# FP4 quantiser of a block kernel: one threshold sum carries the sign sums, half and scale folded together

## The reference, cut to what matters

```python
xn = layernorm(x)                                  # 1024 features
s  = attn_ref(xn, ...)                             # linear attention, projection, MLP 1024 -> 2048 -> 1024
g  = silu(ffn_ref(xn, w_gate, w_up, w_down))       # every operand of the three products is quantised
out = x + s * g

_GRID = [0.0, 0.5, 1.0, 1.5, 2.0, 3.0, 4.0, 6.0]
_MID  = [0.25, 0.75, 1.25, 1.75, 2.5, 3.5, 5.0]
def fp4_quant_dequant(x):                          # blocks of 16 along the last dimension
    scale = max(max|xb| / 6, 1e-12)
    xn = xb / scale
    return _GRID[searchsorted(_MID, |xn|)] * sign(xn) * scale

def ffn_ref(x, w_gate, w_up, w_down):              # 1024 -> 2816 -> 1024
    h = silu(fp4_linear(x, w_gate)) * fp4_linear(x, w_up)
    return fp4_linear(h, w_down)
```

## Time and profile before

| | us |
|---|---|
| median of 2 runs | 6698.14 (6688.92 to 6707.36) |
| profiled execution | 6623.11 |
| its span, slowest core (3) | 6621.5 |
| spans of the other cores | 6599.9 to 6619.9 |
| mean granted TensorE clock, all cores | 0.696 to 0.698 |

### The profile page before, as it was taken

How to read it: one execution, slowest core, us unless ns; L and a number is a source line. 1 busy time by engine, 2 the same in 40 slices (tenths; PEclk the granted TensorE clock), 3 DMA queues, 4 the chain that set the end, 5 groups by cost and what they waited for, 6 DMA issues and landing times.

```text
span 6621.5 us, 58555 instructions; the slowest of 8 cores (6599.9 to 6621.5 us)
## 1 busy us (share of the span) xinstructions
PE 2592.5 (39%) x11098; PEld 1110.6 (17%) x11098; DVE 3878.3 (59%) x8760; ACT 2051.6 (31%) x4067; POOL 3.2 (0%) x13
## 2 busy tenths in 40 slices
PE   0167447642313133374004555522232322223298
PEld 0023113211101011132001222211111111111143
DVE  0500330133787777524987777758888888888522
ACT  0244224321322322222323334323333333333211
POOL 0000000000000000000000000000000000000000
PEclk9999678866656566687556767665666555665599
DMA  9420110014111111001112222230111110111255
GB/s 108 121 61 23 34 50 29 18 46 81 40 42 39 40 35 39 29 24 45 45 54 92 85 92 89 84 89 34 41 44 45 44 44 30 44 45 44 70 194 179
DMA packets 227699, 396.08 MB, mean 60 GB/s; under 512 B 147861, under 2 KB 147989, under 8 KB 217626
## 3 DMA queue, kind: packets, MB, share of 16 engines
q1 hardware_dynamic: 226778, 375.57, 17.6%
q0 software_dynamic: 576, 16.78, 2.3%
HBM read 246.44 MB, written 145.33 MB: 59 GB/s over the span
## 4 chain that ended last, share of the span: by engine, by line
PE 33%; issue 26%; DVE 20%; ACT 11%; SPq 5%; DMA 4%; DVEq 1%; ACTq 0%
PE gps L1093 6%; PE ups L1147 5%; PE kvg_ps L402 4%; PE d_ps L1249 4%; PE c1ps L937 3%; SPq L195 2%; PE c2ps L965 2%; PE q_ps L453 2%; PE prA L601 2%; DVE gld L1159 1%; PE xp4t L1179 1%; DMA xa<-x 1%; PE prB L601 1%; ACT qb_s L709 1%; ACT qb_u L712 1%
## 5 line engine op out<-in xcount | busy, mean ns | idle before, releaser
L1179 PE MATMUL xp4t<-ident_b,hq 128*128 128x128 bf16 x704 | 178.9, 261 | 1306.0 <-ACT hqf L1185 1256.2
L1147 PE MATMUL ups<-wquT,xqu 128*128 128x512 bf16 (+1 forms) x1536 | 364.2, 404 | 71.9 <-DMA xqu<-xqT_h 38.9
L917 PE MATMUL xp2t<-ident_b,xn 128*128 128x128 bf16 x256 | 65.0, 265 | 831.5 <-DVE xn L905 432.1
L1093 PE MATMUL gps<-wqgT,xqf 128*128 128x512 bf16 (+1 forms) x1536 | 377.0, 414 | 19.6 <-ACT xqf L1082 19.6
L1075 PE MATMUL xp3t<-ident_b,xq 128*128 128x128 bf16 x256 | 67.8, 265 | 765.2 <-DVE xq L742 736.1
L703 ACT ACTIVATE qb_sgn<-qb_u 128x704 f32<-128x704 f32 x128 | 101.0, 790 | 839.2 <-DVE qb_u L696 838.2
L362 DVE SCALAR_TENSOR_TENSOR xn<-xn,rstd_all,rep_s 128x1024 bf16<-128x1024 f32 x32 | 41.1, 1284 | 542.7 <-ACT xn L351 481.7
L1249 PE MATMUL d_ps<-wqdT,hln 128*128 128x512 bf16 x1408 | 313.6, 384 | 71.6 <-DMA hln<-hqT_h 54.2
L1159 DVE TENSOR_TENSOR gld<-gld,up 128x2816 f32<-128x2816 f32 x32 | 99.0, 3092 | 372.6 <-ACT up L1156 372.6
L1179 PEld LDWEIGHTS xp4t<-ident_b,hq 128*128 128x128 bf16 x704 | 73.8, 105 | 1409.1 <-issue 1408.3
L402 PE MATMUL kvg_ps<-qkvT,fmsup 128*128 128x512 bf16 x1024 | 275.9, 437 | 23.0 <-ACT fmsup L384 23.0
(11 more groups left out here) (243 smaller groups left out, 6709.8 us busy)
## 6 DMA issues: line engine op xcount, KB each, us to landing
xa<-x SPq DMA_DIRECT2D x160, 512.0 KB, 3.7
gate_h<-gate SPq DMA_DIRECT2D x32, 1408.0 KB, 5.6
gld<-gate_h SPq DMA_DIRECT2D x32, 1408.0 KB, 6.7
hqT_h<-hqf SPq DMA_DIRECT2D x32, 704.0 KB, 3.7
hln<-hqT_h SPq DMA_DIRECT2D x32, 704.0 KB, 5.5
out<-otl SPq DMA_DIRECT2D x32, 512.0 KB, 3.0
winw<-L_ffn_w_gate SPq DMA_DIRECT2D x22, 512.0 KB, 3.4
winw<-L_ffn_w_up SPq DMA_DIRECT2D x22, 512.0 KB, 3.4
```

The lines of the kernel that those rows point to most:

```text
L1093: S.add("pe", lambda pe, b=b, ic=ic, cgo=cgo, cgw=cgw, cgi=cgi: pe.matmul(g_ps[cgi % 4][:, 0:cgw], xqf[b][:, P * ic:P * (ic + 1)], wqgT[:, ...
L1147: S.add("pe", lambda pe, b=b, ic=ic, cgo=cgo, cgw=cgw, cgi=cgi: pe.matmul(u_ps[cgi % 4][:, 0:cgw], xqu[b][:, P * ic:P * (ic + 1)], wquT[:, ...
L1179: S.add("pe", lambda pe, b=b, ic=ic: pe.transpose(xp4_ps[ic % 2], hq[b][:, P * ic:P * (ic + 1)], ident_b[:]), waits=tw, inc="PE", ev="a2_t ...
```

## The change

Inside `quant_gen` only. The two sign instructions on VectorE (`sadd`, `smul`) move ahead of the four threshold counts. `smul` now forms s5+s6+2*s7. The first count, a `tensor_scalar`, becomes a `scalar_tensor_tensor` that adds this sum. The instruction that joined the counts with the sum (`tA3`) is gone. The factor one half goes into the product of sign and scale, which becomes a `scalar_tensor_tensor`, and the last instruction adds 4 instead of 2. Per unit VectorE has 8 instructions behind `u2` instead of 9, and a weight chunk has 30 steps instead of 31. Nothing changes on ScalarE, TensorE or in the DMAs.

```diff
@@ -712,8 +712,14 @@
             S.add("sc", lambda sc: sc.activation(s7, u2, AF.Sign, bias=thrB[:, 2:3]),
                   waits=[e("sgn")], inc="SC", ev=e("s7"))
             yield
-            S.add("v", lambda v: v.tensor_scalar(tA, u2, 0.0625, None, op.is_gt),
-                  waits=[e("u2")], inc="V", ev=e("tA1"))
+            S.add("v", lambda v: v.tensor_tensor(s5, s5, s6, op.add),
+                  waits=[e("s5"), e("s6")], inc="V", ev=e("sadd"))
+            yield
+            S.add("v", lambda v: v.scalar_tensor_tensor(s6, s7, 2.0, s5, op.mult, op.add),
+                  waits=[e("s7"), e("sadd")], inc="V", ev=e("smul"))
+            yield
+            S.add("v", lambda v: v.scalar_tensor_tensor(tA, u2, 0.0625, s6, op.is_gt, op.add),
+                  waits=[e("u2"), e("smul")], inc="V", ev=e("tA1"))
             yield
             S.add("v", lambda v: v.scalar_tensor_tensor(tB, u2, 0.5625, tA, op.is_gt, op.add),
                   waits=[e("tA1")], inc="V", ev=e("tB1"))
@@ -724,22 +730,13 @@
             S.add("v", lambda v: v.scalar_tensor_tensor(tB, u2, 3.0625, tA, op.is_gt, op.add),
                   waits=[e("tA2")], inc="V", ev=e("tB2"))
             yield
-            S.add("v", lambda v: v.tensor_tensor(s5, s5, s6, op.add),
-                  waits=[e("s5"), e("s6")], inc="V", ev=e("sadd"))
-            yield
-            S.add("v", lambda v: v.scalar_tensor_tensor(s6, s5, 0.5, s7, op.mult, op.add),
-                  waits=[e("s7"), e("sadd")], inc="V", ev=e("smul"))
-            yield
-            S.add("v", lambda v: v.scalar_tensor_tensor(tA, tB, 0.5, s6, op.mult, op.add),
-                  waits=[e("smul")], inc="V", ev=e("tA3"))
-            yield
             sb_ = sca.rearrange("p nb -> p nb ()").broadcast_to([P, nb, 16])
-            S.add("v", lambda v: v.tensor_tensor(
-                tB.rearrange("p (nb b) -> p nb b", b=16),
-                sgn.rearrange("p (nb b) -> p nb b", b=16), sb_, op.mult),
-                waits=[e("sgn"), e("tA3")], inc="V", ev=e("tBs"))
-            yield
-            S.add("v", lambda v: v.scalar_tensor_tensor(dst_ap, tA, 2.0, tB, op.add, op.mult),
+            S.add("v", lambda v: v.scalar_tensor_tensor(
+                tA.rearrange("p (nb b) -> p nb b", b=16),
+                sgn.rearrange("p (nb b) -> p nb b", b=16), 0.5, sb_, op.mult, op.mult),
+                waits=[e("sgn"), e("tB2")], inc="V", ev=e("tBs"))
+            yield
+            S.add("v", lambda v: v.scalar_tensor_tensor(dst_ap, tB, 4.0, tA, op.add, op.mult),
                   waits=[e("tBs")], inc="V", ev=done_ev)
 
         def run_gens(gens):
```

More of the change, by code:

```diff
@@ L726, in quant_gen @@
             yield
-            S.add("v", lambda v: v.tensor_tensor(s5, s5, s6, op.add),
-                  waits=[e("s5"), e("s6")], inc="V", ev=e("sadd"))
-            yield
-            S.add("v", lambda v: v.scalar_tensor_tensor(s6, s5, 0.5, s7, op.mult, op.add),
-                  waits=[e("s7"), e("sadd")], inc="V", ev=e("smul"))
-            yield
-            S.add("v", lambda v: v.scalar_tensor_tensor(tA, tB, 0.5, s6, op.mult, op.add),
-                  waits=[e("smul")], inc="V", ev=e("tA3"))
-            yield
-            sb_ = sca.rearrange("p nb -> p nb ()").broadcast_to([P, nb, 16])
-            S.add("v", lambda v: v.tensor_tensor(
-                tB.rearrange("p (nb b) -> p nb b", b=16),
-                sgn.rearrange("p (nb b) -> p nb b", b=16), sb_, op.mult),
-                waits=[e("sgn"), e("tA3")], inc="V", ev=e("tBs"))
-            yield
-            S.add("v", lambda v: v.scalar_tensor_tensor(dst_ap, tA, 2.0, tB, op.add, op.mult),
+            sb_ = sca.rearrange("p nb -> p nb ()").broadcast_to([P, nb, 16])
+            S.add("v", lambda v: v.scalar_tensor_tensor(
+                tA.rearrange("p (nb b) -> p nb b", b=16),
+                sgn.rearrange("p (nb b) -> p nb b", b=16), 0.5, sb_, op.mult, op.mult),
+                waits=[e("sgn"), e("tB2")], inc="V", ev=e("tBs"))
+            yield
+            S.add("v", lambda v: v.scalar_tensor_tensor(dst_ap, tB, 4.0, tA, op.add, op.mult),
                   waits=[e("tBs")], inc="V", ev=done_ev)
```

## The result

The changed kernel takes 6971.99 us in the median (6880.50 to 7012.17, 11 runs), the kernel before, run beside it, 6698.14 (10 runs, 6622.97 to 6779.58). The ratio is 1.0412, 95% interval 1.0324 to 1.0501. In some executions of either kernel the cores of one die or of both run at a lower granted clock and take longer, and the ratios leave the clearly longer ones out while the medians hold them all. Two more sets of runs of the same pair gave 1.0372 (1.0313 to 1.0431) and 1.0311 (1.0240 to 1.0382); the mean of the three, weighted by their intervals, is 1.036, some 240 us. The forecast was 224 us, a ratio of 1.033, 6922 us, with 6870 to 6968 as its range. Direction and mechanism were right, and so was the size of what the quantiser's stages lose; the two medians of this set are 274 us apart, and the changed kernel's lies 4 us above the range.

A forecast was written before the change was run, and what follows sets the result against it. No engine bounds the whole; loops of waits between engines set the gate and up stages, VectorE the weight and MLP stages. 18 + 36 + 113 + 57 = +224 us on 6698 gives 6922 us, range 6870 to 6968.

The forecast's parts named there:

- The gate stage: Gate stage: six more instructions of 0.604 us behind the sign sum's wait, 3.62 us a tile, +113 us in all.
- the bare stall: Quantiser pairs: VectorE waits at the sign sum for ScalarE's Signs, 1.99 us per 704 pair, 1.68 per 512 pair.
- the ring: Gate stage loop: sign sums and following VectorE work, transposes, matmuls, Silus, Signs; the early counts sat free in VectorE's wait.
- The up stage: Up stage: the first pair of 32 tiles pays 1.12 us net each, +36 us.
- the cover of the second pair: Up stage: the second pair's 1.12 us hides in 9.63 us of idle time; uncovered it would add another 36.
- rival 3: TensorE's clock: longer pauses slow all gate matmuls, +26 us, as much again in the up stage; 6974 us, chance 6%.
- The weight stage: Weight stage: all 16 pairs lie on the path and pay 1.12 us net each, +18 us.
- The MLP stage: MLP stage with chunks: 44 pairs at 1.1 us, +49, plus shifted portion ends; together +57 us.
- 15 counted places: MLP stage: 30-step chunks shift where portions end; terms +20, +8, -12, -3 and -6 us.
- Rival 1: Quantiser: Signs are ready in time, so the shorter VectorE program wins 72 us; 6626 us, chance 3%.
- Rival 2: Gate stage: the loop has slack, so the six extra instructions cost nothing, 112 us drop out; 6810 us, chance 5%.
- the last one: Whole kernel: adds 224 us to the runs' median 6698, 76 us above the profiled span of 6621.5, giving 6922.

The follow-up runs named there:

- gate_stage_only: Against the kernel before: the changed order in the gate stage's quantiser alone, the old one elsewhere; gate stage 910.7 us (+113.7).
- product_first: Against the changed kernel: same eight instructions, product of sign and scale put ahead of the sign sums; ratio to the kernel before 1.0042.
- arrival_order: Against the kernel before: counts stay ahead, then the product of sign and scale, then s5, s6, s7 added one by one as they arrive; ratio 0.9938.
- load_ahead_new: both_rings_open_new plus x of tile t+2 loaded ahead of tile t's stores in the gate stage; 6359.04 us, kernel before 6737.22.
- both_rings_open_new: Changed kernel with gate Signs ahead of the previous tile's Silus and up-stage transposes and copies ahead of the next tile's product and quantiser; ratio 0.9852.
- whole_again: The changed kernel run once more, unaltered, for a second profile and ratio against the kernel before; 6915.09 us, ratio 1.0372.
- moved_only: Against the kernel before: only the two sign instructions moved ahead of the counts, all nine instructions and the old arithmetic kept; ratio 1.0492.
- load_ahead_old: both_rings_open_old plus x of tile t+2 loaded ahead of tile t's stores in the gate stage; 6116.55 us, kernel before 6737.22.
- both_rings_open_old: Kernel before with gate Signs ahead of the previous tile's Silus and up-stage transposes and copies ahead of the next tile's product and quantiser; ratio 0.9536.
- all_but_gate: Against the kernel before: the changed order everywhere except in the gate stage's quantiser; ratio 1.0164.
- signs_before_silu_old: Kernel before with the gate stage's quantiser of tile t+1 put ahead of tile t's matmuls and Silus; ratio 1.0001, gate stage 789.1 us.

## Why the prediction was right, and where it was not

**The gate stage** (+113 computed, +113.4 to +113.8 measured) held in each step: the sum waits for ScalarE in 32 of 32 tiles, 331 us against "some 320", tiles 29.0 us apart as written, and the sum's start still set by the Signs. `gate_stage_only` shows the term by itself, `product_first` and `arrival_order` that it goes by the instructions behind the wait, `load_ahead_new` that it falls to the bare stall when the ring is opened.

**The up stage** (+36 computed, +45 measured). The stall (1.91 us, computed 1.99) and its net price (1.18 for 1.12 a tile) were right, and so was the cover of the second pair, shown by `both_rings_open_new`. The under-sized part lies ahead of the product: from the first `ups` matmul to the product a tile takes 12.10 us in place of 11.84, 8 us over the stage. The rows of the `ups` matmuls have 364.2 us busy, 404 ns each, before and 373.3, 411 ns, in the first profile after: TensorE's matmuls themselves. This is rival 3 with a small price: I had ruled that the mix of clock levels would stay, and in the gate stage it did (a burst of 48 is 11.78 us in the mean in both kernels). In the up stage it did not: over the 32 bursts of core 3 the granted clock was 0.84 in the mean before, 0.83 in `whole_again` and 0.79 in `moved_only`, and the bursts took 11.38, 11.59 and 12.13 us.

**The weight stage** (+18 computed, +19.4): 30.5 us of waits in 16 pairs, "16 x 2.0 = 32" was expected.

**The MLP stage** (+57 computed, +50.2 measured) was a sum of 44 plain stalls (49) and of 15 counted places where a portion ends (8 net; the terms as written add up to 56, not 57). The total is inside the 40 to 80 that I had set as its test, but no run took one counted place by itself. The plain stalls alone would give 49. `moved_only`, whose chunks keep their 31 steps, grew by 80.8 here; less the 44 removed L715 (44 x 0.68 = 30) that is 51, what the changed kernel grew by. This speaks for places that came to nothing in the sum; whether my count is right in its parts is open.

**The rivals.** Rival 1 (the shorter program wins) needed the `s6` ready within 0.87 us and found it 1.9 late; it becomes true in the up and weight stages of `product_first`, where other work stands in front of the wait. The Trainium skill (Perfetto Trace Analysis, "Identifying the Most-Contended Engine") tells to optimise the engine of highest occupancy first. Here that engine had 104 us less to do and the kernel took some 240 us longer; `load_ahead_old`, with VectorE's work as before (3870 us busy), took 513 us less than the 4910 between attention and down by having waits taken away. Rival 2 fell with the gate stage.

**VectorE's busy time** fell by 104 us, not 134. I had scaled up the busy times of L715's rows, 0.95 and 0.75 us a pair, but each pair overlaps the start of the next one: by their steps in the timeline (0.87 and 0.68 us a pair, which the path's sums used) it is 80 x 0.87 + 76 x 0.68 = 121. The last 17 us are not accounted for.

**The step that failed is the last one**: "The median of the runs is 76 us above that span; I add the same 224 to it", and with it the upper end of the range, 6968, which holds 26 us for the clock and 20 for the MLP count and nothing for the spread of the runs (the lower end has 9). The 224 held, and the base happened to hold: the kernel before, run beside the changed one, has the very median of 6698.14 that the sum started from. What did not hold is that the changed kernel's median would lie the same 76 us above the span that the sum gives: in this set it lies 127 us above the computed 6845, though the profiled spans of `whole_again` (6818.5 to 6863.8 on its cores) are where the sum puts them. That the base was right was luck: the two runs I had, 6688.92 and 6707.36, are among those ten and happen to be the middle two, and they lay close together by chance. In five sets of runs the median of the kernel before was 6653.57, 6669.51, 6698.14, 6730.79 and 6737.22, and its single executions went from 6617 to 6799, and the changed kernel's medians were 6915.09, 6959.86 and 6971.99. The medians of the two kernels were 274, 246 and 229 us apart in the three sets in which both ran. So a median of seven to 25 executions moves by about 40 us to either side, and the range allowed 9 and 0. With 40 us to either side beside its own terms (42 below, 46 above) it would have been 6840 to 7008. A large part of the time that moves between executions is in stages without the quantiser; the profile after happened to show it:

Down stage and attention after, core 1 and then core 3 (stretch, its length, busy time of PE, PEld, DVE, ACT and POOL, granted clock, DMA share, GB/s):

```profile
0.00:930.00 930.00, 374.60 (x1631) 154.55 (x1631) 217.91 (x344) 241.25 (x478) 3.19 (x13) 0.88 0.34 68
6480.00:6889.00 409.00, 360.52 (x1408) 149.43 (x1408) 78.42 (x64) 64.55 (x96) 0.00 (x0) 0.82 0.52 166
```

```profile
0.00:930.00 930.00, 395.83 (x1567) 156.93 (x1567) 200.84 (x319) 230.86 (x456) 3.19 (x13) 0.82 0.33 65
6480.00:6889.00 409.00, 316.79 (x1430) 138.96 (x1430) 80.36 (x67) 70.44 (x118) 0.00 (x0) 0.92 0.55 177
```

and the down stage of the kernel before, core 3:

```profile
6262.00:6621.00 359.00, 313.64 (x1408) 137.57 (x1408) 78.41 (x64) 64.58 (x96) 0.00 (x0) 0.96 0.53 184
```

The same 1408 matmuls of the down stage take 360.5 us on core 1 at a granted 0.82 and 313.6 before at 0.96. In this execution cores 2 to 5 have the low clock in attention (0.82, stage 915 to 929 us) and cores 0, 1, 6 and 7 in the down stage (0.79 to 0.84, 379 to 388 us): each core loses 25 to 40 us at one place or the other, cores 4 and 5 some 10 to 15 us at the second place too. The stages with the quantiser can be hit as well: in the profile of `load_ahead_new` the MLP stage took 1899.8 and 1911.7 us on cores 0 and 1, at a granted 0.61 (1500 to 3100 us), and 1842.7 to 1847.5 on the other six, at 0.65 or 0.66.

**What stays open** is whether the changed order brings such episodes about more often. For it: the first profile of the changed kernel has one on all 8 cores, `whole_again` a slight one on some (down 361 to 368 us on three cores), the two profiles of the kernel before none on 16 cores. Against it: `both_rings_open_old`, with the quantiser of before, has them on four cores (912 to 915 us in attention on cores 4 and 5, 361 to 365 in down on cores 6 and 7) and `arrival_order`, with the counts in their old place, on cores 2 and 3 (945 to 947 in attention); `gate_stage_only` has them on four cores (939 to 940 in attention, 380 to 384 in down) and `all_but_gate`, with half of the change's cost, on none; the timed executions of the kernel before spread as far (6617 to 6799) as the changed kernel's (6849 to 7022). The excess of the measured 240 over the 228 of the stages is inside the interval of the ratios, and the undisturbed dies differ by 225 and 230, so nothing needs to be explained by it.

## What to carry to other kernels

Before an instruction that waits for another engine is moved up, ask two things: how late is what it waits for at the new place, and what stands behind it on its engine that used to stand in front. Independent work in front of a wait is worth its length, so four "free" counts in front of a 5.7 us wait cost 3.6 us a tile when they go behind it, and one covering pair of instructions brought nearly half of that back there and all of the loss in two other stages. When a ring is opened, look at every queue that it passes, the one that issues DMAs too, for who is late next; and when a prediction is made from one profile, its range needs the spread of the runs as well as that of the terms.

## What the runs showed of the hardware

**The matmuls of a dense stage took 15% longer in the mean on some cores (360.5 us busy for 313.6), not on others.** Core 1 in the down stage after, TensorE, against core 3 at the same time:

```profile
6618.36 24.43 PE L1246 MATMUL d_ps<-wqdT,hln 128*128 128x512 bf16 x88 [2.78 <-DMA hln<-hqT_h]
```

```profile
6621.25 19.15 PE L1246 MATMUL d_ps<-wqdT,hln 128*128 128x512 bf16 x88 [2.28 <-ACT sfl L1258]
```

278 ns for a matmul of 512 columns and 218; both engines had been in the same dense stage for over 100 us, and the second is the 2.4 GHz level. The slower one lies between the 1.2 and the 2.4 GHz level. A little later the granted clock holds still, on core 1 and then on core 3 (stretch, length, TensorE's busy time and matmuls, granted clock, DMA share, GB/s):

```profile
6700.00:6750.00 50.00, 50.00 (x193) 0.81 0.53 185
```

```profile
6700.00:6750.00 50.00, 45.12 (x207) 1.00 0.55 192
```

From 6650 to 6850 us cores 0 and 1 have 0.81 in each stretch of 50 us, cores 6 and 7 0.81 to 0.84, and the other four 0.97 to 1.00. It comes in pairs of cores here: 0 and 1 with 6 and 7, in `gate_stage_only` 4 and 5 in down and 6 and 7 in attention, in `load_ahead_new` 0 and 1 in attention and 2 and 3 in down. The Trainium skill (TensorE: Matmul & The Clock Gate, "Seeing it yourself") names a peak-current limit that takes a whole die to 13/16 of the clock once three of its cores run dense matmuls, and holds it there while they do.
**The same matmuls in two bursts took longer than in one.** In the up stage a matmul of `ups` took 404 ns in the mean before and 457 with both rings open (436.0 us busy in place of 364.2), though the stage was 311 us shorter. Before, a tile's 48 matmuls are one burst; with both rings open the last 16 wait for ScalarE's copy and then run near the 1.2 GHz level. One tile of each kernel, core 3:

```profile
5099.70 10.88 PE L1147 MATMUL ups<-wquT,xqu 128*128 128x512 bf16 x48
```

```profile
5003.60 9.56 PE L1170 MATMUL ups<-wquT,xqu 128*128 128x512 bf16 x32
5034.59 5.10 PE L1170 MATMUL ups<-wquT,xqu 128*128 128x512 bf16 x16 [21.44 <-ACT up L1179]
```

The granted clock in these three bursts was 0.89, 0.74 and 0.53. That the stage is denser is not the reason: the gate stage of `load_ahead_old` (595.8 us in place of 797) keeps its 48 in one burst and takes 413 ns a matmul (414 before), while in `signs_before_silu_old` it is split into 32 and 16 and takes 452. In the up stage with both rings open VectorE's time hides these 72 us; in a ring they would be a loss, which no run here tried.
